# 32-row score tiles in a first attention, gate rows by way of DRAM in the last experts, and the first front of those experts moved into the attention before them

## The reference

```
L0 attention: 16 heads of 8, causal; scores * 8**-0.5 clipped to +-10, softmax, values, out projection
L0 experts:   8 experts, F = 256, top 2 of x @ Wg.T, softmax over the two;
              y = sum_e gate_e * ((silu(x W1_e) * (x W2_e)) W3_e)
L1 attention: 16 heads of 8, not causal, rotary embedding on q and k, softmax, values, projection + bias
L1 experts:   router softmax(gelu(x rW1 + rb1) rW2 + rb2) over 4 experts, top 2;
              y = sum_e combine_e * (gelu(x We1_e + be1_e) We2_e + be2_e), hidden width 512
```

## Time and profile before

| | us |
|---|---|
| median of 3 runs | 1720.16 (1710.94 to 1721.71) |
| the profiled execution: its time | 1729.45 |
| its span, first to last instruction | 1727.2 |
| busy: TensorE, VectorE, ScalarE, GpSimd | 1566.1, 1410.2, 1167.6, 108.6 |
| mean granted TensorE clock | 0.953 of 2.4 GHz |

### The profile page before, as it was taken

The page is one execution under the profiler, slowest core; times in us unless marked ns, Lnnn a source line. Parts: engine busy times, 40 slices in busy tenths (PEclk is TensorE's granted clock), DMA queues, the critical chain, the costliest instruction groups (busy, mean ns, idle before and its releaser), DMA issues.

```text
span 1727.2 us, 32148 instructions
## 1 busy us (share of the span) xinstructions
PE 1566.1 (91%) x11104; PEld 801.1 (46%) x11104; DVE 1410.2 (82%) x2503; ACT 1167.6 (68%) x1779; POOL 108.6 (6%) x187
## 2 busy tenths in 40 slices
PE   6899999969999999968999999999999978888887
PEld 3433333346656655633333333333333336666665
DVE  3688999867777777777999999999999827887777
ACT  3798999833333333215999999999999966655565
POOL 2000000000100111020000000000000000010000
PEclk9898999989999999975999999999999989999999
DMA  7482222222322221240111111111111010000100
GB/s 214 146 234 85 91 91 92 69 69 63 100 100 91 71 83 62 91 154 3 44 38 48 54 37 38 37 43 37 42 54 43 18 39 14 20 21 26 34 7 13
DMA packets 68461, 112.97 MB, mean 65 GB/s; under 512 B 23088, under 2 KB 32176, under 8 KB 67712
## 3 DMA queue, kind: packets, MB, share of 16 engines
q1 hardware_dynamic: 68352, 111.48, 20.6%
HBM read 67.79 MB, written 43.65 MB: 65 GB/s over the span
## 4 chain that ended last, share of the span: by engine, by line
PE 57%; DVE 19%; issue 9%; ACT 6%; DMA 4%; SPq 3%; POOL 1%; ACTq 0%; DVEq 0%; POOLq 0%
PE full_o L731 14%; PE max_pair L702 11%; PE causal_o L459 6%; PE hid_pair L1028 6%; PE triple L443 6%; PE score L716 3%; DVE negmax_h L816 3%; PE bank L1119 2%; DVE hid L1435 2%; DVE lin_u L1431 2%; ACT cprobs L487 1%; PE bank L1131 1%; DMA k_scr<-qk_hi 1%; DVE st L1263 1%; PE hid_pair L960 1%
## 5 line engine op out<-in xcount | busy, mean ns | idle before, releaser
L816 DVE TENSOR_REDUCE negmax_h<-max_pair 128x2 f32<-128x1024 f32 x512 | 588.3, 1217 | 23.4 <-PE max_pair L702 23.3
L782 ACT ACTIVATE probs<-score 128x512 f32<-128x512 f32 x1024 | 547.2, 596 | 78.6 <-PE score L716 59.2
L731 PE MATMUL full_o<-probs,v_st 128*32 128x256 f32 x4096 | 330.8, 395 | 17.7 <-ACT o_sb L790 17.7
L716 PE MATMUL score<-q_st,k_st 32*128 32x512 f32 x1024 | 316.6, 503 | 0.8 <-ACT probs L782 0.7
L487 ACT ACTIVATE cprobs<-triple 128x1536 f32<-128x1536 f32 x192 | 265.7, 1454 | 22.6 <-PE triple L443 19.9
L702 PE MATMUL max_pair<-k_st,q_st 32*128 32x512 f32 x1024 | 264.2, 515 | 10.9 <-DVE negmax_h L816 9.6
L1225 ACT ACTIVATE act_s<-hid_pair 128x512 f32<-128x512 f32 x128 | 76.5, 597 | 192.6 <-PE hid_pair L1028 192.5
L702 PEld LDWEIGHTS max_pair<-k_st,q_st 32*128 32x128 f32 x1024 | 97.6, 188 | 234.4 <-DVE negmax_h L816 179.9
L1028 PE MATMUL hid_pair<-x_hi,w_hi 128*128 128x512 f32 x384 | 198.8, 518 | 6.8 <-ACT act_s L1230 6.8
L517 DVE TENSOR_SCALAR cprobs<-cprobs 128x1536 f32<-128x1536 f32 (+6 forms) x272 | 163.5, 625 | 0.4 <-ACT cprobs L487 0.4
L459 PE MATMUL causal_o<-cprobs,v_st 128*32 128x512 f32 (+3 forms) x1536 | 157.6, 507 | 3.2 <-DVE cprobs L517 3.2
(11 more groups left out here) (139 smaller groups left out, 1631.4 us busy)
## 6 DMA issues: line engine op xcount, KB each, us to landing
o_scr<-o_sb SPq DMA_DIRECT2D x64, 256.0 KB, 2.1
gate_all<-gate_scr SPq DMA_DIRECT2D x32, 512.0 KB, 5.6
k_st<-k_scr SPq DMA_DIRECT2D x64, 128.0 KB, 2.8
q_st<-q_scr SPq DMA_DIRECT2D x128, 64.0 KB, 2.4
q_st<-q_scr SPq DMA_DIRECT2D x16, 512.0 KB
k_st<-k_scr SPq DMA_DIRECT2D x64, 104.0 KB
q_scr<-qk_hi SPq DMA_DIRECT2D x24, 256.0 KB, 4.1
k_scr<-qk_hi SPq DMA_DIRECT2D x24, 256.0 KB, 4.2
```

Source lines behind the costliest of these rows:

```text
L716: nc.tensor.matmul(sbank[L.score_bank(e)][:, :], k_st[p][rows, j, kt * P:(kt + 1) * P], q_st[p][rows, q0:q0 + w], start=True, stop=True, t ...
L731: last = nc.tensor.matmul(full_o[SLOT * j:SLOT * (j + 1), cols], v_st[p][:, kt, j, :], probs[s % NP][:, j, cols], start=(kt == 0 and part ...
L782: nc.scalar.activation(probs[s % NP][:, L.HEADS[j], :], sbank[L.score_bank(e)][:, :], ACT.Exp, scale=SCALE).then_inc(L.exp_done, 1)
L816: nc.vector.tensor_reduce(negmax_h[:, qt // TPC, half, heads[0]:heads[1] + 1:2, qt % TPC], ring[slot][:, :, :], AXX, ALU.max, negate=True) ...
```

## The change

- **32-row tiles.** `k_st` becomes as wide as a sequence, and each head's score matmul in the first attention takes its own 32 rows. The clears of `k_st` and the stored pads go; in the second attention matmuls take 24 rows (pairs) or 26 (scores), with the ones set once by GpSimd after the first attention. The "twins" pieces now join the two chunks' blocks of one head, and stand after the first full block of chunk 1. The save of chunk 0 moves from slot 5 to 7, and its last block from slot 3 to 5.
- **Room.** With the smaller stacks `w_hi` and `w_lo` have memory of their own, and GpSimd rounds the weights during the attentions: two copies and two subtractions of 128x2048, one a round, in rounds 10 to 13 of the first and 2 to 5 of the second.
- **Loads.** Weights are loaded after the loads of rounds 5, 6 and 8; the first stacks of the second attention in chunks 2 and 3 of the first experts, with eight DMAs for each round in place of five; the raw weights of the last experts in round 0 of the second attention. GpSimd, not VectorE, fills `v_st` for it.
- **Gates of the last experts** go to DRAM and back as in the first ones. A chunk's gates are transposed at its own step 2 and copied at ScalarE's step 3; VectorE first needs them at its step 6. ScalarE's exp becomes `e ** x` on GpSimd, and the matmuls with `expert_row` and their copies go.
- **The plan** of the last experts: projection at step 2 in place of 4, norm 4 in place of 6, router 12 in place of 11, and so on; four hidden banks in place of three.
- **The first front** of the last experts runs in the last round of the second attention: TensorE's projection, transpose, hidden layer and router after steps 3, 7, 9 and 12, ScalarE's two gelus after step 10, VectorE's and GpSimd's parts as they come. After the round TensorE goes on with the first hidden matmuls.

```diff
-    SAVE_PREV, SAVE_0 = 1, 5
+    SAVE_PREV, SAVE_0 = 1, 7
     def __init__(self, sem):
         self.n = 0
+        twins = [("twins", [(qc, qc * TPC + 2, j, 2 * P * qc, 2 * P) for qc in range(CPB)]) for j in self.HEADS]
...
             for kt in range(d):
                 pieces += [("full", [(qc, kt, j, 0, CH)]) for j in self.HEADS]
+                if kt == 0:
+                    pieces += twins
             pieces += [("first", [(qc, d, j, 0, CH)]) for j in self.HEADS]
             pieces += [("edges", [(qc, d + 3, j, 0, P), (qc, d + 1, j, P, 3 * P)]) for j in self.HEADS]
-            pieces += [("twins", [(qc, d + 2, j, 0, 2 * P), (qc, d + 2, j + 1, 2 * P, 2 * P)]) for j in (0, 2)]
         self.slots = [pieces[k:k + 3] for k in range(0, len(pieces), 3)]
         self.N = len(self.slots)
         assert len(pieces) == 3 * self.N and self.N % 2 == 0 and self.N % CP == 0
-        self.last_kt = [qc * TPC + 2 for qc in range(CPB)]
+        self.last_kt = [2, KT - 1]
...
-                r, rows = rows_of(j)
-                last = nc.tensor.matmul(triple[n % 2][:, bk, off:off + w], k_st[p][rows, j, kt * P:(kt + 1) * P],
+                r, rows = slot_rows(j, SLOT)
+                last = nc.tensor.matmul(triple[n % 2][:, bk, off:off + w], k_st[p][rows, kt * P:(kt + 1) * P],
...
+        def pool_round_weights(layer, k, lower):
+            if lower:
+                nc.gpsimd.tensor_tensor(w_lo[k][:, :], w_raw[k][:, :], w_hi[k][:, :].bitcast(F32),
+                                        ALU.subtract).then_inc(w_lower, 1)
+            else:
+                nc.gpsimd.tensor_copy(w_hi[k][:, :], w_raw[k][:, :]).then_inc(w_upper, 1)
+        def pool_weights(pool, layer, n):
+            k = n // 2
+            if n % 2 == 0:
+                pool.wait_ge(raw_loaded[k], 16 * (layer + 1))
+            else:
+                pool.wait_ge(w_upper, 2 * layer + k + 1)
+            pool_round_weights(layer, k, n % 2 == 1)
+        WEIGHTS_FROM = 10
         def pool_causal(pool, L):
-            for p in range(2):
-                nc.gpsimd.memset(k_st[p][:, :, :].bitcast(F32), 0.0).then_inc(L.zeroed, 1)
-            nc.gpsimd.memset(pad_rows[:, :], 0.0).then_inc(pads_set, 1)
             pool.wait_ge(stages[0].v_saved, 2 + CPB)
             pool_first_values(pool, L)
-            pool.wait_ge(stages[0].v_saved, 2 * B + 2)
-            pool.wait_ge(pads_stored, 16 * DK)
-            nc.gpsimd.memset(pad_rows[:, :], 1.0).then_inc(pads_set, 1)
-            pool_next_values(pool, L)
+            for i in range(NG - 2):
+                pool.wait_ge(L.pv_done, L.values_before(i + 1))
+                pool_stage_v(pool, L, i + 2, i % 2)
+                if 0 <= i - WEIGHTS_FROM < 4:
+                    pool_weights(pool, 0, i - WEIGHTS_FROM)
+            pool.wait_ge(L.scores_ready, L.N * NG)
+            for p in range(2):
+                nc.gpsimd.memset(k_st[p][:, :].bitcast(F32), 1.0).then_inc(layers[1].ones_set, 1)
...
-            sp_store_pads(sp)
...
+            for i in range(4, NG - 2):
+                next_round(i, i % 2)
+                if i == 5:
+                    for t, name in WEIGHTS:
+                        sp.dma_start(t[tuple(slice(None) for _ in t.shape)], d[name]).then_inc(w_loaded, 16)
+                    sp.dma_start(b_o1[:, :], d["b_o1"].broadcast_to([P, D])).then_inc(w_loaded, 16)
+                    sp.dma_start(rb2[:, :], d["rb2"].broadcast_to([P, E1])).then_inc(w_loaded, 16)
+                if i == 6:
+                    for k, name in enumerate(("w1", "w2")):
+                        sp.dma_start(w_raw[k][:, :], d[name]).then_inc(raw_loaded[k], 16)
+                if i == 8:
+                    sp.dma_start(rope_a[:, :], d["rope_a"]).then_inc(rope_loaded, 16)
+                    sp.dma_start(rope_b[:, :], d["rope_b"]).then_inc(rope_loaded, 16)
...
+                if not nxt:
+                    pe_early_front(pe, L, s)
...
+                if not nxt and s == RH_AT:
+                    act_beside(act, stages[2], plan[1].hidden, None, 0, 0, 1)
...
+                if 0 <= i - 2 < 4:
+                    pool_weights(pool, 1, i - 2)
...
+                for st_, scr in ((k_st[p], k_scr1), (q_st[p], q_scr1)):
+                    sp.dma_start(st_[r:r + HALVES, :].bitcast(F32),
+                                 scr[bass.ds(b, 1), bass.ds(g * HG + j, 1), :, :].rearrange("b h c n -> (b h) c n")
+                                 ).then_inc(L.stacks_loaded[p], 16)
...
-                          (plan[1], (3, 5, None, None, None, None, 1, 4, 6, 8, 10, 11, 12, 15))):
+                          (plan[1], (4, 6, None, None, None, None, 1, 2, 4, 8, 10, 12, 13, None))):
...
+        GATES_AT = 2
+        EARLY = (3, 7, 9, 12)
+        EARLY_STEPS = {s: [n] for s, n in zip(EARLY, (plan[1].o_proj, plan[1].x_turn, plan[1].hidden, plan[1].router))}
+        RH_AT = 10
         n_exp = [E0, E1]
-        h_banks, h_lead = [2, 3], [1, 3]
-        y_bank = [bank[0][:, :], hbank[3]]
-        h_of = [[n % 2 for n in range(SPC)], [n % 3 if n < SPC - 1 else 1 for n in range(SPC)]]
-        h_apart = [[2] * SPC, [2 if n in (1, SPC - 1) else 3 for n in range(SPC)]]
+        h_banks, h_lead = [2, 4], [1, 3]
+        y_bank = [bank[0][:, :], bank[1][:, :]]
...
-            nc.tensor.matmul(bank[1][:, :], expert_row[:, e, :], gate_t[:, :], start=True,
-                             stop=True).then_inc(st.gbc_ready, 1)
+        def front_banks(layer, front):
+            if layer == 1 and front == 0:
+                return hbank[0], hbank[1]
+            return bank[2][:, :], bank[3][:, :]
...
+        def pe_turn_gates(pe, st, f):
+            pe.wait_ge(st.gates, f + 1)
+            for t in range(TPC):
+                last = nc.tensor.transpose(bank[3][0:E0, slice_of(t)], gts[:, 0, t, :], ident[:, :])
+            last.then_inc(st.gates_turned, 1)
...
+                if layer == 1 and n == GATES_AT:
+                    pe_turn_gates(pe, st, c)
...
+        def pe_first_hidden(pe, st, layer):
             pe.wait_ge(w_lower, 2 * (layer + 1))
             for n in range(h_lead[layer]):
                 pe_hidden(pe, st, 0, 0, n, layer)
+        def pe_early_front(pe, L, s):
+            st = stages[2]
+            if s == EARLY[0]:
+                pe.wait_ge(L.ring_free, PAIRS * NG)
+            for n in EARLY_STEPS.get(s, ()):
+                pe_beside(pe, st, n, None, 0, 0, 1)
+        def pe_end(pe, st, layer):
+            if layer == 0:
+                for n in range(SPC):
+                    pe_beside(pe, st, n, None, 0, 0, layer)
+            else:
+                pe.wait_ge(st.gate_pre, 1)
+            pe_first_hidden(pe, st, layer)
...
-                        nc.scalar.activation(e_sm[:, :, :], sc8[:, :, 0:E1], ACT.Exp).then_inc(st.gate_exp, 1)
...
+        def act_save_gates(act, st, f):
+            act.wait_ge(st.gates_turned, f + 1)
+            wait_used(act, st.gates_kept, 16 * f)
+            nc.scalar.activation(gate_rows[:, :], bank[3][0:E0, :], ACT.Copy).then_inc(st.gate_t, 1)
...
-            nc.scalar.activation(gate_bc[e % 2], bank[1][:, :], ACT.Copy).then_inc(st.gbc_saved, 1)
...
+                    if n == GATES_AT + 1:
+                        act_save_gates(act, st, c)
...
-                if n == plan[layer].o_turn:
-                    for k in range(2):
-                        act.wait_ge(raw_loaded[k], 16 * (layer + 1))
-                        act.wait_ge(layers[layer].o_saved, CPB * NG)
-                        nc.scalar.activation(w_hi[k][:, :], w_raw[k][:, :], ACT.Copy).then_inc(w_upper, 1)
+            act.wait_ge(w_lower, 2 * (layer + 1))
...
-            ch.link(nc.vector.tensor_copy(g_halves[:, :, 0:E0].bitcast(F32R), gts[:, 0, :, :]))
-            nc.vector.tensor_tensor(g_halves[:, :, E0:2 * E0].bitcast(F32R), gts[:, 0, :, :], g_halves[:, :, 0:E0],
...
-                if n == (pl.o_turn - 1 if layer == 1 or front == 0 else pl.g_turn + 1):
+                if n == (pl.o_turn - 1 if front == 0 else 10):
...
+                    if layer == 1 and front == 0:
+                        dve.wait_ge(st.x_turned, 1)
+                        nc.vector.tensor_copy(xt[0][:, :], hbank[1]).then_inc(st.xt_ready, 1)
+                        nc.vector.tensor_copy(x_hi[0][:, :], hbank[1]).then_inc(st.x_upper, 1)
...
-            dve.wait_ge(st.gbc_saved, 1 + c * E1 + e + 1)
+            dve.wait_ge(st.gate_in[e // 2], 16 * (c + 1))
...
+            dve.wait_ge(w_lower, 2 * (layer + 1))
             for n in range(SPC):
                 dve_beside(dve, st, n, None, 0, 0, layer)
-                if n == plan[layer].norm:
-                    for k in range(2):
-                        dve.wait_ge(w_upper, 2 * layer + k + 1)
-                        nc.vector.tensor_tensor(w_lo[k][:, :], w_raw[k][:, :], w_hi[k][:, :].bitcast(F32),
-                                                ALU.subtract).then_inc(w_lower, 1)
             if layer == 0:
```

(34 more changed lines are left out.)

294 lines of the change are left out of this document (99 added, 195 removed).

## The result

The changed kernel takes **1982.17 us** (median of 4 runs, 1972.24 to 1989.31) against 1720.93 for the kernel before (1710.94 to 1722.03): 1.152 times as long, 95% interval 1.147 to 1.158. The forecast was 1666. The profiled execution has a span of 1987.5 us; before it had 1727.2.

A forecast was written before the change was run, and what follows sets the result against it. First attention: three engines near full; second: VectorE; last experts: none full. Terms -5, -2, -0.5, -17.3, -29 sum to -54: 1729.45 to 1675.5, then 1666 as the runs' median lies 9.3 lower; range 1650 to 1682 (0.53).

The forecast's parts named there:

- rounding beside it: Second attention: GpSimd's rounding meets VectorE reductions that read PSUM, one input; 0 us (bounds 0 and +4).
- raw weights passing: Second attention: 2 MB of raw weights pass shortly before round 1's maxima; 0 to +2 us.
- the term of the chunks: Last experts: removed work and waits take a chunk from 36.1 to 32.5 us; -29 over eight chunks (bounds -44, -9).
- First attention: First attention: 32-row tiles -4, q_st stall -6, rounding on GpSimd +5; sum -5 us (bounds -15.7 and +17).
- The stall behind the loads: First attention: ScalarE's stall behind a load of q_st goes as other loads move later; 6 us gained (bounds 3 and 7.5).
- The rounding: First attention: GpSimd's four operations may hold VectorE's clips, partly absorbed by scores issued four slots ahead; +5 us (bounds 0 and 20).
- the rival that has VectorE stand through them: First attention: VectorE stands through all 20 us of GpSimd's rounding, +15, total 1681 us; chance 0.07.
- First experts and transition: First experts: x_lo and gates come earlier, -2 us; change to second attention: GpSimd's clear of k_st goes, -0.5.
- Early front: Before the last experts: 24.8 us go, last round of second attention grows 7.5; -17.3 us (bounds -21 and -15.6).
- the pow's stall: Last experts: GpSimd's pow takes 3.6 us a chunk, about 2 under VectorE's step between, leaving 1.6 of stall.
- Gate rows late: Last experts: VectorE waits for gate rows sent through DRAM; at 8 us a chunk the total is 1730; chance 0.04.
- the signs named: Last round 39 to 43 us; chunks 31.5 to 33.5, VectorE over 88%; exp idle under 0.35 a round; four stretched slots.

The follow-up runs named there:

- e2: The kernel before with only the second attention's tiles cut to 24-row pairs and 26-row scores: 2017.22 us, 1.169 of before.
- e1: The changed kernel with full 32-row pair and score tiles put back in the second attention: 1699.69 us, 0.985 of before.
- e7: e1 with weights, raw matrices and rope tables loaded behind the loads of round 3 again: 1696.35 us, 0.984 of before.
- e10: e9 with the first attention's two rounding subtractions moved from GpSimd to VectorE, one piece a round in rounds 8 to 15: 1664.18 us, 0.965.
- e8: e1 with each of GpSimd's rounding subtractions cut into eight pieces: 1697.10 us, 0.984 of before.
- e17: e1 with the early front's matmuls and gelus behind the last round of the second attention again: 1704.64 us, 0.987 of before.
- e18: e1 with the last experts' gate exp on ScalarE again in place of the pow on GpSimd: 1680.14 us, 0.976 of before.
- e5: e1 with o_proj and norm of the last experts one step later (3 and 5): 1682.01 us, 0.976 of before.
- e15: The changed kernel with 32-row pairs and scores in rounds 0 to 4 of the second attention, 24 and 26 rows after: median 1703.57 us.
- e11: e1 with 24-row pairs from round 5 of the second attention on, scores 32 rows throughout: 1693.87 us, measured once.
- e9: e1 with the edits of e5 and e6 together: 1672.07 us, 0.971 of before.
- e6: e1 with VectorE's steps that use the pow in the last experts one step later: 1690.28 us, 0.980 of before.
- e3: e1 with 26-row score tiles in the second attention, pairs at 32 rows: 1712.35 us, measured once.

## Why the prediction was wrong

**The step that failed** is one that the prediction does not have. It costed the second attention by its neighbours (rounding beside it, raw weights passing): "0 (bounds 0 and +4)" and "0 to +2". The diff also cuts the rows that its 2048 pair and score matmuls read, from 32 to 24 and 26. No term stands for that: it was put at nothing without a reason, and the clock was not asked about. The rows of before held the warning: the stage is entered at half clock and the prediction saw 0.98 over it without asking what ends the low stretch. Shown by e2 (tiles alone: 1.169 times) and e1 (tiles put back: 0.985). The whole 261 us and, with 1982.17 - 1699.69 = 282, some more is this step; the rest of the change gains 1.5%. That is not the 54 us either: 1699.69 lies 34 us over the forecast, and what fails there is above all the term of the chunks, -29 forecast and +2.4 measured.

Why the rows of a tile weigh on the granted clock is not shown. The Trainium skill (TensorE: Matmul & The Clock Gate, Part 1) says that the clock follows how busy TensorE has been of late. By that, a TensorE that is 99% busy for 914.8 us would not be held at half; the trace of the changed kernel shows that it is, and the measurement decides.

**The other terms**, read from e1 and its edits:
- *First attention, forecast -5*: measured -11.5 (after) and -15.7 (e1). Twelve exps (a round) without a stall take 17.27 us before and 16.12 in e1, 1.15 less, some 18 us in sixteen rounds, where I took 4 and allowed 8.2 at most. I took ScalarE's own pace as 1.41 us an exp from eight in 11.28, and so only the 0.51 us of idle time a round as open; but without a break it is faster. A lone exp takes 1.45 us (at 261.75 in e1), and in a run the next starts before the last has ended:

```profile
149.22 36.72 ACT L482 ACTIVATE cprobs<-triple 128x1536 f32<-128x1536 f32 x27
```

  That is 1.36 each, and 192 times 0.05 is 9.6 us that I had booked as work. The 32-row tiles and the new order of the pieces were not tried apart. The stall behind the loads: forecast 6; in the kernel before the twelve exps around it take 24.72 us, 7.5 over its usual round, and e1 has none of it; undoing the move of the loads alone brings back 2.6 (e7), so that something else in the change has a part in it; what, was not tried. The rounding: forecast +5. The four rounds beside it are 5.3, 5.1, 0.7 and 0.5 us over 16.12, 11.5 in all; ScalarE stood 9.9 us for the two subtractions (4.17, 0.88, 4.09, 0.77), and e10 gained 7.9 from moving them. GpSimd's four operations last 12.9 us together (4.54, 4.53 and twice 1.90), not the 20 of the upper bound, so nearly all of their time was paid: the rival that has VectorE stand through them was right in kind, and the slots of lead, by which I took half of each subtraction as absorbed, absorbed next to nothing. The Trainium skill (SBUF — State Buffer, "SBUF: two separate sides") has this as an exclusive lock; the 4.86 us agree, and e8 shows that shorter operations do not soften it.
- *First experts and transition, forecast -2.5*: -2.2 in after, +0.2 in e1. The other traces, of kernels that do not differ from e1 in this stretch, have 441.3 to 447.1 us, and e2, which does not differ from before in it, 445.1 against 448.1. Not told apart.
- *Early front, forecast -17.3*: -4.6 us by e17. The last round became 13.5 us longer in place of 7.5; the half clock of 13.7 us behind ScalarE's leave was not in the sum. And the gap was not all the front's: from the last save of o_sb to the first act_s the kernel before took 27.6 us and e17, with the front in the gap again, takes 21.1. The 6.5 between them fit the rounding of the weights, which the kernel before had there on ScalarE and VectorE; that was not tried alone.
- *Chunks, forecast -29*: +2.4 in e1. The terms removed are gone (no table load, no wait for xs or g_halves), but VectorE's idle time stayed, 8.2 us of 37.5. I had priced the pow's stall at 1.6 and it is 2.1; what I missed is what stands behind a stall. The pow costs 16.6 us over eight chunks (e18), the early o_proj 24.1 (e5). The sentence "as norm comes two steps earlier" was counted as a gain only; that o_proj, moved from step 4 to 2 for it, now comes before its ot is ready, and that turn, copy and gelus queue behind it in order, was not followed. It is the question that I had set myself only for the gate rows.
- *Gate rows late*, the slower rival: VectorE does not wait for gate_all once in e1's last experts, and once for 1.3 us in the changed kernel's. The slower side came from elsewhere.

Of the signs named: the hidden matmuls do start with the end of the last values (1394.92 in e1), no load is in the chain of the first attention, and outside the four rounds of the rounding exps stand at most 0.27 us at a time behind the first ten us. A slot stretched by 2 us or more in two rounds, not four. One sign of being wrong did come: a clip stood for the whole of a GpSimd operation. The last round (47.8, not 39 to 43), the chunks (37.5, not 31.5 to 33.5) and VectorE's share (78%, not 88) were wrong in e1 too.

## What to carry to other kernels

Put the granted clock beside every stage that is entered at half, and ask of each edit to its matmuls, shape included, whether the clock still comes back; where it might not, keep the wide tiles for the first rounds (e15), or throughout, as here the narrow ones gained nothing (e1). A step that is moved earlier in an in-order queue is to be checked for its own input first: what stands behind it waits too, on each engine in turn. And a stall on VectorE or ScalarE of 2 to 4 us is not its own length: where TensorE stood 3.47 us for it in e1's last round, 13.7 us of half clock came with it, and they are part of the price. The version to keep is e10, 1664.18 us, 3.5% under the kernel before; the exp on ScalarE (e18) together with it was not tried.

## What the runs showed of the hardware

- A pair matmul of 24 rows takes the same 495 ns at full clock as one of 32 (groups of e1 from 784 to 1340, and of e11 from 1000 to 1360, in this order):

```profile
L701 PE MATMUL max_pair<-k_st,q_st 32*128 32x512 f32 x938 | 233.6, 495 | 1.2
```

```profile
L701 PE MATMUL max_pair<-k_st,q_st 24*128 24x512 f32 x584 | 145.5, 495 | 0.9
```

  Yet under 24-row pairs a half clock stayed at half, with TensorE 99% busy for up to 928 us (e2), in 23 of 24 executions; a full clock stayed full under them for 417 us in e11, and in e15 for 388 us with 26-row scores beside them.
- The entry at half clock varies from run to run with 32-row pairs: 34.1 us (e1, e8, e9, e11, e18), 37.5 (e17), 41.0 (e7), 47.8 (before), 54.6 (e6, e10), 61.4 (e5, e15), and 85.3 with 26-row scores (e3). The stage is then 621.4 us at 34.1 (e1), 628.1 at 54.6 (e6) and 629.5 at 61.4 (e5), about 0.3 us for each at half.
- A pow of 128x16 on GpSimd takes 2.91 to 3.13 us, one of 128x4 1.03 to 1.45, more than half of them 1.04 (e1).
- GpSimd's copy of 128x2048, one input, takes 1.9 us and cost the round beside it 0.5 to 0.7 us; its subtraction, two inputs, takes 4.54 and cost 5.1 to 5.3.
